# Where GpSimd subtracts the first feed-forward weights inside a tile of the first attention

## The chip, the cores and the metric

The kernel runs on one core of one Trainium2 chip. The metric is the device time of one execution in microseconds (us). The core has TensorE (PE, matrix products and transposes), VectorE (DVE), ScalarE (ACT), GpSimd (POOL) and SyncE (SP, which here issues most DMAs). Each engine runs its own instructions in order. Engines meet only through semaphores.

## The reference, cut to what matters

The network has four parts, each added to the residual `x` of 2048 rows by 512 columns. The change lies in the first, and the weights that it prepares belong to the second:

```
features_n = rmsnorm(features, fn_w)                 # features: ctx, 2048 x 512
Q = text @ Wq_w.T + Wq_b ;  K = features_n @ Wk_w.T + Wk_b
Q, K = rmsnorm(Q, qn_w), rmsnorm(K, kn_w)            # x += softmax(Q K^T * scale) features_n
inter = xf @ c1_w.T @ c2_w.T                         # second part: the largest of each 32 is chosen
h = relu(w1[chosen] . xf) ;  x += h @ w2t[chosen]
```

Products are made in about twice the precision of one pass: each operand is held as a high and a low part, and three products are added, high by high, low by high and high by low. So every operand needs a low part, which is the raw value minus its high part. `w1`, the first weights of the second part, are 128 x 7168 numbers in the laid-out form. They are split in eight pieces of 128 x 896 while the first attention runs.

## The kernel before, in words

The first attention goes over 16 tiles of 128 rows (n = 0 to 15). In tile n the engines finish the scores of tile n and prepare tiles n+1 and n+2. The instruction order of each engine is written out by hand in a `body(n)` for each. No scheduler moves anything.

A tile turns around the key of the next tile, as follows.

- TensorE projects the key and the query of tile n+1 (lines 72 to 74, 24 products of 512 columns), makes the scores of tile n (12 products), transposes rows (L881), attends for tile n-1, transposes the query (L907) and then the key (L913), and the probabilities (L969).
- VectorE adds the key bias (L688, into `kb`), the query bias (L692), makes scores and their maximum (L715, L717), and then `scale_keys` (L696): `kn = kb * krs * wqk`. Its two large inputs `kb` (in `a_wide`) and `wqk` (in `shared`) both lie in SBUF. `krs` is one number per row. L913 transposes `kn`, so it waits for L696.
- ScalarE makes the sum of squares of the key (L532), the exponentials (L579) and the high parts, those of `w1` at L560 and L564, one piece in each of tiles 7 to 14. L499 makes sums of squares for later roots.
- GpSimd makes the three roots of a tile (`tile_roots`, L400, L402, L406), the low part of the transposed features (L416), the key root `krs` (`key_root`, L379 and L381), then waits for `kn` (`s_kn`). After that come the low part of the features (`features_lo`, L411, which reads `cw` and `f_hi`), the weighting of the features (`weigh`, L374) and, in tiles 8 to 15, one subtraction of a piece of `w1` (`split_w1`, L456: 128 x 896 out of two SBUF inputs, float32 minus float16). Tile 9 has two small root instructions for a later layer norm (L114, L116) ahead of `features_lo`.

In tiles 8 to 13 the subtraction L456 is the last instruction of GpSimd's tile. In tile 14 it stands behind the wait for `kn` and ahead of `features_lo`. In tile 15 it follows the roots, since that tile has no key of a next one. Piece s is subtracted in tile s + 8, and its high part was made by ScalarE in tile s + 7.

In the trace tile 8 starts on GpSimd at 102.92 us and the last subtraction of `w1` ends at 170.12 us. The rest of the program, up to 1487 us, follows in order.

Of the kernel before, what the change touches and what calls it, by code (L numbers as in the profile page):

```python
# [33 lines left out]
NT = ROWS // P  # L34
# [155 lines left out]
def l0_attention(nc, ctx, big_ctx, m, prep, fw, a):  # L190
# [82 lines left out]
    SPLIT_AT = {n: n - 7 for n in range(7, 15)}  # L273
# [82 lines left out]
    def pool_steps(pool):  # L356
# [11 lines left out]
        def weigh(n):  # L368
            pool.wait_ge(c_in_, (n + 1) * 16)
            if n:  # L370
                pool.wait_ge(s_fl, n)
            else:
                pool.wait_ge(bq_fnw_in, 32)
            pool.tensor_tensor(cw[:, :], craw[:, bass.ts(n % 2, D)], fnw, ALU.mult).then_inc(s_cw, 1)  # L374
# [3 lines left out]
        def root(out, mean, down, eps, done):  # L378
            pool.tensor_scalar(out, mean, down, eps, ALU.mult, ALU.add).then_inc(s_rve, 1)  # L379
            pool.wait_ge(s_rve, next(roots))  # L380
            pool.tensor_tensor(out, out, m.neg_half[:, 0:1], ALU.pow).then_inc(done, 1)  # L381
# [11 lines left out]
        def tile_roots(n):  # L393
            pool.wait_ge(s_qss, n + 1)
            pool.wait_ge(s_css, min(n + 3, NT))
            pool.wait_ge(s_ve, 2 * min(n + 4, NT))
            if n >= RING:
                pool.wait_ge(s_pTl, n - 1)
            three = root4[:, n % RING, :]
            pool.tensor_tensor(three, sums[:, 1:4], eps3[:, :], ALU.add).then_inc(s_rve, 1)  # L400
            pool.wait_ge(s_rve, next(roots))
            pool.tensor_tensor(three, three, m.neg_half[:, 0:3], ALU.pow).then_inc(s_rve, 1)  # L402
            pool.wait_ge(s_rve, next(roots))
            if n >= 2:
                pool.wait_ge(s_xn, min(n + 2, NT))
            pool.tensor_scalar(sh2[:, (n + 3) % 2:(n + 3) % 2 + 1], sums[:, 0:1], -1.0, three[:, 0:1], ALU.mult, ALU.mult)\  # L406
                .then_inc(s_root, 1)

        def features_lo(n):
            pool.wait_ge(s_f, n + 1)  # L410
            pool.tensor_tensor(f_lo[:, bass.ts(n % F_RING, D)], cw[:, :], f_hi[:, bass.ts(n % F_RING, D)],  # L411
                               ALU.subtract).then_inc(s_fl, 1)

        def features_T(n):
            pool.wait_ge(s_cTh, n + 1)
            pool.tensor_tensor(cT_lo[:, :, :], cT_raw[n % 2][:, :, :], cT_hi[:, :, :], ALU.subtract).then_inc(s_cTl, 1)  # L416

        def key_root(n):
            pool.wait_ge(s_kss, n + 1)
            if n:  # L420
                pool.wait_ge(s_kn, n)
            root(krs[:, :], kss[:, :], 1.0, L0_EPS, s_krs)

        def body(n, first=False, ahead=True, project=True):
            if first:
                key_root(1)
            tile_roots(n)
            if ahead:
                features_T(n + 2)
            if first:  # L430
                weigh(1)
            if project:
                if not first:
                    key_root(n + 1)
                pool.wait_ge(s_kn, n + 2)
            if n == ROOT_AT:
                prep.pool_rstd(pool, 0)
            if n == NT - 2:
                split_w1(SPLIT_AT[n - 1])
            if project:  # L440
                features_lo(n + 1)
            if ahead:
                weigh(n + 2)
            if n - 1 in SPLIT_AT and n != NT - 2:
                split_w1(SPLIT_AT[n - 1])
            if n == C_AT:
                split_c1()
            if n == C_AT + 1:
                split_c2(0)
            if n == NT - 1:  # L450
                split_c2(1)

        def split_w1(s):
            cols = bass.ts(s, W1P // 2)
            pool.wait_ge(w1h_ok, s + 1)
            pool.tensor_tensor(fw.w1_lo[:, cols], w1_piece(s), fw.w1_hi[:, cols], ALU.subtract).then_inc(w1l_ok, 1)  # L456
# [15 lines left out]
        def split_c1():  # L472
            pool.wait_ge(ch_ok, 1)
            pool.tensor_tensor(fw.c1_lo[:, :, :], fw.c1_raw[:, :, :], fw.c1_hi[:, :, :], ALU.subtract).then_inc(cl_ok, 1)

        def split_c2(half):
            cols = bass.ts(half, INTER // 2)
            pool.wait_ge(ch_ok, 2)
            pool.wait_ge(cl_ok, half + 1)
            if half:  # L480
                pool.wait_ge(w1l_ok, 8)
            else:
                pool.wait_ge(s_cw, C_AT + 4)
            pool.tensor_tensor(fw.c2st[64:96, cols], fw.c2_raw[64:96, cols], fw.c2st[64:96, cols], ALU.subtract)\
                .then_inc(cl_ok, 1)
            pool.wait_ge(cl_ok, half + 2)

        run(body)(pool)

    def act_steps(act, before_exps):  # L490
# [2390 lines left out]
```

## Time and profile before

| | us |
|---|---|
| median of 3 runs (lowest, highest) | 1486.43 (1485.72, 1488.51) |
| the profiled execution | 1488.97 |
| its span, first to last instruction | 1487.2 |
| PE busy | 1456.9 (98%) |
| DVE busy | 1121.6 (75%) |
| ACT busy | 793.4 (53%) |
| POOL busy | 708.2 (48%) |
| mean granted TensorE clock | 0.999 of full speed |

The 1.8 us between the profiled execution's time and its span lie before the first and behind the last instruction. The shares are those of the whole span. The change touches a stretch of about 68 us out of 1487, and what its instructions wait for has to be read in that stretch.

### The profile page before, as it was taken

How to read it: one execution, taken by the hardware profiler on the slowest of the kernel's cores; microseconds unless marked ns; L12 is line 12 of the kernel's file. 1: busy time of each engine (PE TensorE's matmuls, PEld its weight loads, DVE VectorE, ACT ScalarE, POOL GpSimd, SP SyncE). 2: the span in 40 equal slices, each digit the busy share in tenths (PEclk: the TensorE clock that was granted, in tenths of full speed). 3: DMA queues.
4: the chain of work that ended last, by engine and by line, in shares of the span. 5: the costliest groups of instructions: out<-in, count | busy, mean ns of one | idle time of the engine just before them, and what ended most of it. 6: DMA issues, size and time to landing. Idle time of an engine off the chain costs nothing.

```text
span 1487.2 us, 27765 instructions
## 1 busy us (share of the span) xinstructions
PE 1456.9 (98%) x9948; PEld 851.1 (57%) x9948; DVE 1121.6 (75%) x2161; ACT 793.4 (53%) x3201; POOL 708.2 (48%) x668
## 2 busy tenths in 40 slices
PE   8999999999999989999999999999999999999998
PEld 6888645555555555556555555655555565555554
DVE  5887787888877878676776776777677677677868
ACT  5678731211123776565556646655754664565663
POOL 6678885554665453344233434333343433343553
PEclk9999999999999999999999999999999999999999
DMA  5744445443444585534443543543454345234523
GB/s 191 239 150 141 128 90 116 106 94 82 75 82 72 118 167 90 125 86 76 110 79 66 108 99 54 102 89 78 89 93 89 82 84 106 51 66 70 103 48 114
DMA packets 359225, 148.98 MB, mean 100 GB/s; under 512 B 342336, under 2 KB 342720, under 8 KB 356144
## 3 DMA queue, kind: packets, MB, share of 16 engines
q1 hardware_dynamic: 357792, 139.87, 44.2%
q10 hardware_dynamic: 1296, 7.34, 1.5%
q8 instruction: 79, 1.29, 0.4%
q14 instruction: 58, 0.48, 0.1%
HBM read 60.11 MB, written 4.19 MB: 43 GB/s over the span
## 4 chain that ended last, share of the span: by engine, by line
PE 49%; DVE 6%; ACT 5%; POOL 3%; DMA 2%; SPq 1%; issue 1%; DVEq 0%; POOLq 0%; ACTq 0%
PE bank L72 16%; PE bank L73 15%; PE bank L74 15%; ACT a_prob L1977 3%; PE bank L2649 2%; DMA a_kT_lo<-a_kn_lo 2%; ACT a_oT_lo L1954 1%; POOL a_qrs L1849 1%; DVE a_oT_lo L2246 1%; ACT a_qr_hi L1951 1%; POOL a_prob L1831 1%; DVE a_kn L2201 1%; DVE a_qve L2185 1%; DVE x_res L2169 1%; DVE x_res L2333 1%
## 5 line engine op out<-in xcount | busy, mean ns | idle before, releaser
L1977 ACT ACTIVATE a_prob<-a_prob,a_nmx 128x64 f32<-128x64 f32 x512 | 170.2, 334 | 250.0 <-DVE a_nmx L2222 249.9
L1831 POOL TENSOR_TENSOR a_prob<-a_prob,a_mask 128x512 f32<-128x512 f32 x64 | 79.9, 1269 | 278.4 <-DVE a_prob L2216 278.4
L72 PE MATMUL bank<-w,xT_hi 128*128 128x448 f16 (+1 forms) x512 | 187.5, 366 | 1.1 <-PEq L1043 1.1
L74 PE MATMUL bank<-w,xT_hi 128*128 128x448 f16 (+1 forms) x512 | 187.3, 366 | 0.0
L73 PE MATMUL bank<-w,xT_lo 128*128 128x448 f16 (+1 forms) x512 | 187.2, 366 | 0.0
L1849 POOL TENSOR_TENSOR a_qrs<-a_qve,neg_half 128x8 f32<-128x8 f32 x64 | 104.2, 1645 | 138.9 <-DVE a_qve L2185 138.6
L1251 ACT CAST f_h_hi<-h 128x448 f16<-128x448 f32 x64 | 35.6, 563 | 207.2 <-DVE h L1325 207.1
L2169 DVE SCALAR_TENSOR_TENSOR x_res<-bank,a_oinv,x_res 128x512 f32<-128x512 f32 x128 | 95.4, 746 | 64.2 <-PE bank L74 64.2
L2174 DVE SCALAR_TENSOR_TENSOR a_qr_lo<-bank,a_qr_hi 128x512 f16<-128x512 f32 x128 | 87.9, 687 | 46.4 <-ACT a_oT_lo L1954 27.4
L1837 POOL TENSOR_TENSOR a_p_hi<-a_prob,a_rden 128x512 f16<-128x512 f32 x64 | 69.5, 1086 | 104.3 <-DVE a_rden L2230 104.3
L1189 POOL TENSOR_TENSOR f_h_lo<-h,f_h_hi 128x448 f16<-128x448 f32 x64 | 72.8, 1141 | 88.9 <-ACT f_h_hi L1251 88.9
L72 PE MATMUL bank<-w,a_cT_hi 128*128 128x256 f16 x384 | 104.7, 273 | 1.0 <-DVE a_qr_lo L2174 1.0
L73 PE MATMUL bank<-w,a_cT_lo 128*128 128x256 f16 x384 | 104.7, 273 | 0.0
L74 PE MATMUL bank<-w,a_cT_hi 128*128 128x256 f16 x384 | 104.7, 273 | 0.0
L1954 ACT ACTIVATE a_oT_lo<-bank 128x128 bf16<-128x128 f32 x400 | 103.8, 282 | 0.0
L72 PE MATMUL bank<-w,a_oT_hi 128*128 128x512 f16 x256 | 97.2, 380 | 0.8 <-DVE x_res L2169 0.8
L73 PE MATMUL bank<-w,a_xT_lo 128*128 128x512 f16 x256 | 97.5, 381 | 0.0
L72 PE MATMUL bank<-w,a_xT_hi 128*128 128x512 f16 x256 | 97.5, 381 | 0.0
L74 PE MATMUL bank<-w,a_xT_hi 128*128 128x512 f16 x256 | 97.4, 381 | 0.0
L72 PE MATMUL bank<-shared,a_oT_hi 128*128 128x512 f16 x256 | 97.2, 380 | 0.1
L1998 ACT ACTIVATE a_oT_hi<-bank 128x512 f16<-128x512 f32 x97 | 54.3, 596 | 80.1 <-PE bank L74 59.1
L73 PE MATMUL bank<-w,a_oT_lo 128*128 128x512 f16 x256 | 97.0, 379 | 0.0
(355 smaller groups left out, 4439.3 us busy)
## 6 DMA issues: line engine op xcount, KB each, us to landing
shared<-in_l_wq SPq DMA_DIRECT2D x8, 1024.0 KB, 4.9
shared<-in_l_wo SPq DMA_DIRECT2D x8, 1024.0 KB, 5.2
shared<-in_w ACTq DMA_DIRECT2D x8, 896.0 KB, 4.7
craw<-in_w SPq DMA_DIRECT2D x11, 512.0 KB, 3.8
a_wide<-in_l_ctxT SPq DMA_DIRECT2D x16, 256.0 KB, 4.0
x_res<-in_x SPq DMA_DIRECT2D x16, 256.0 KB, 4.4
shared<-in_ctx SPq DMA_DIRECT2D x16, 256.0 KB, 4.3
shared<-in_l_wkv SPq DMA_DIRECT2D x8, 512.0 KB, 4.0
```

What stands on the lines that cost most here:

```text
L72: pe.matmul(out, a_hi, b_hi, start=first, stop=False)
L73: pe.matmul(out, a_lo, b_hi, start=False, stop=False)
L74: return pe.matmul(out, a_hi, b_lo, start=False, stop=last)
L1189: pool.tensor_tensor(h_lo[:, quarter(q)], h[:, quarter(q)], h_hi[:, quarter(q)], ALU.subtract).then_inc(s_hl, 1)
L1831: pool.tensor_tensor(blocks(prob[u][:, :]), blocks(prob[u][:, :]), mask[:, :].unsqueeze(1).broadcast_to([P, NB, S]), ALU.add).then_inc(s_m ...
L1837: pool.tensor_tensor(blocks(p_hi[u][:, :]), blocks(prob[u][:, :]), share, ALU.mult).then_inc(s_ph, 1)
L1849: pool.tensor_tensor(qrs[:, half], qve[:, half], m.neg_half[:, half], ALU.pow).then_inc(s_qrs, 1)
L1954: ins = act.activation(scratch, q_banks[t][:, h * HD:(h + 1) * HD], ACT.Square, scale=SUM_DOWN, accum_out=qss[:, h % 2, t, h // 2:h // 2 + 1])
L1977: ins = act.activation(pt, pt, ACT.Exp, bias=nmx[:, col:col + 1], accum_out=den[:, col:col + 1])
L1998: ins = act.activation(oT_hi[:, u * NB:(u + 1) * NB, b * S:(b + 1) * S], blocks(pv_banks[u][b][:, :]), ACT.Copy, scale=OUT_DOWN)
L2169: dve.scalar_tensor_tensor(xt, banks[t % 2][:, :], oinv[i // NCH % 2][:, c:c + 1], xt, ALU.mult, ALU.add).then_inc(s_x, 1)
L2174: dve.scalar_tensor_tensor(qr_lo[:, t, :], q_banks[t][:, :], SUM_DOWN, qr_hi[:, t, :], ALU.mult, ALU.subtract).then_inc(s_ql, 1)
```

## The change

In tiles 8 to 14 GpSimd makes its subtraction of `w1` right behind the key root, ahead of the wait for `kn`. The piece, its operands and its size are the same. Tile 15 keeps its order. No other engine's code is changed.

```diff
             if project:
                 if not first:
                     key_root(n + 1)
+            if n - 1 in SPLIT_AT:
+                split_w1(SPLIT_AT[n - 1])
+            if project:
                 pool.wait_ge(s_kn, n + 2)
             if n == ROOT_AT:
                 prep.pool_rstd(pool, 0)
-            if n == NT - 2:
-                split_w1(SPLIT_AT[n - 1])
             if project:
                 features_lo(n + 1)
             if ahead:
                 weigh(n + 2)
-            if n - 1 in SPLIT_AT and n != NT - 2:
-                split_w1(SPLIT_AT[n - 1])
```

GpSimd's order in tile 11, one of the six tiles 8 to 13, before. In brackets are the semaphores that an instruction waits for: `a0_kn_ok` is `s_kn`, `a0_w1_hi_ok` says that the high part of `w1` is there.

```order
L379 TENSOR_SCALAR a_krs<-a_kss 128x1 [waits a0_kn_ok,a0_kss_ok]
L381 TENSOR_TENSOR a_krs<-a_krs,neg_half 128x1 [waits a0_root_input]
L411 TENSOR_TENSOR a_big<-a_wide,a_big 128x512 [waits a0_f_ok,a0_kn_ok]
L374 TENSOR_TENSOR a_wide<-shared 128x512 [waits a0_f_lo_ok,a0_ctx_in]
L456 TENSOR_TENSOR w<-shared,w 128x896 [waits a0_w1_hi_ok]
L400 TENSOR_TENSOR a_root<-a_sums,a_eps 128x3 [waits a0_ln_var_steps,a0_pT_ok,a0_css_ok,a0_qss_ok]
```

The same place in the changed kernel, where the lines behind the change are numbered one lower:

```order
L379 TENSOR_SCALAR a_krs<-a_kss 128x1 [waits a0_kn_ok,a0_kss_ok]
L381 TENSOR_TENSOR a_krs<-a_krs,neg_half 128x1 [waits a0_root_input]
L455 TENSOR_TENSOR w<-shared,w 128x896 [waits a0_w1_hi_ok]
L411 TENSOR_TENSOR a_big<-a_wide,a_big 128x512 [waits a0_f_ok,a0_kn_ok]
L374 TENSOR_TENSOR a_wide<-shared 128x512 [waits a0_f_lo_ok,a0_ctx_in]
L400 TENSOR_TENSOR a_root<-a_sums,a_eps 128x3 [waits a0_ln_var_steps,a0_pT_ok,a0_css_ok,a0_qss_ok]
```

The subtraction moved from behind L374 to directly behind L381, and the wait for `kn` now stands behind it, on L411. In tile 14 GpSimd's order before was this:

```order
L379 TENSOR_SCALAR a_krs<-a_kss 128x1 [waits a0_kn_ok,a0_kss_ok]
L381 TENSOR_TENSOR a_krs<-a_krs,neg_half 128x1 [waits a0_root_input]
L456 TENSOR_TENSOR w<-shared,w 128x896 [waits a0_w1_hi_ok,a0_kn_ok]
L411 TENSOR_TENSOR a_big<-a_wide,a_big 128x512 [waits a0_f_ok]
L400 TENSOR_TENSOR a_root<-a_sums,a_eps 128x3 [waits a0_ln_var_steps,a0_pT_ok,a0_css_ok,a0_qss_ok]
```

Now it is this:

```order
L379 TENSOR_SCALAR a_krs<-a_kss 128x1 [waits a0_kn_ok,a0_kss_ok]
L381 TENSOR_TENSOR a_krs<-a_krs,neg_half 128x1 [waits a0_root_input]
L455 TENSOR_TENSOR w<-shared,w 128x896 [waits a0_w1_hi_ok]
L411 TENSOR_TENSOR a_big<-a_wide,a_big 128x512 [waits a0_f_ok,a0_kn_ok]
L400 TENSOR_TENSOR a_root<-a_sums,a_eps 128x3 [waits a0_ln_var_steps,a0_pT_ok,a0_css_ok,a0_qss_ok]
```

Here only the wait moved, from the subtraction to the instruction behind it.

## Rows read from the trace of the kernel before

**Rows 1.** Busy time in tile 12: us, then busy us of each engine.
```profile
142.80:152.30 9.50, 9.50 (x58) 8.17 (x57) 7.80 (x15) 8.92 (x20) 7.77 (x10) 1.00 0.36 104
```

**Rows 2.** Waits between 95 and 172 us: total, times, longest.
```profile
PE bank L913 <- DVE a_wide L696: 3.0, 4, 1.2
```

**Rows 3.** Timeline of tile 12: start, duration, engine, line [idle before it].
```profile
144.48 0.56 POOL L381 TENSOR_TENSOR a_krs<-a_krs,neg_half 128x1 f32<-128x1 f32 x1
...
145.08 0.75 DVE L696 SCALAR_TENSOR_TENSOR a_wide<-a_wide,a_krs,shared 128x512 f32<-128x512 f32 x1
...
145.34 0.60 PE L907 MATMUL bank<-ident,a_wide 128*128 128x128 f32 x4
...
145.88 0.66 PE L913 MATMUL bank<-ident,a_wide 128*128 128x128 f32 x4
145.91 1.28 POOL L411 TENSOR_TENSOR a_big<-a_wide,a_big 128x512 fp32r<-128x512 f32 x1 [0.86 <-DVE a_wide L696]
...
150.87 0.20 POOL L400 TENSOR_TENSOR a_root<-a_sums,a_eps 128x3 f32<-128x3 f32 x1 [0.36 <-issue]
```

**Rows 4.** Line 1319, all 64: duration ns min/median/max.
```profile
L1319 DVE TENSOR_TENSOR a_wide<-a_wide x64: 624/626/1252, 178.9 to 477.3; 128x448 bf16<-128x448 bf16 x64
```

**Rows 5.** Timeline of GpSimd and VectorE near 180 us.
```profile
179.12 2.53 POOL L1183 TENSOR_TENSOR f_w_lo<-shared,f_w_hi 128x1024 f16<-128x1024 f32 x1
...
180.87 1.25 DVE L1319 TENSOR_TENSOR a_wide<-a_wide 128x448 bf16<-128x448 bf16 x1
```

**Rows 6.** Line 851, all four: duration ns min/median/max.
```profile
L851 DVE TENSOR_TENSOR a_big<-x_res,a_big x4: 680/682/1786, 11.2 to 16.8; 128x512 fp32r<-128x512 f32 x4
```

**Rows 7.** Timeline of GpSimd at the start of the program.
```profile
16.39 1.67 POOL L416 TENSOR_TENSOR a_big<-a_wide,a_big 128x512 fp32r<-128x512 f32 x1 [1.42 <-ACT a_big L524]
...
22.97 0.55 POOL L381 TENSOR_TENSOR a_first_crs<-a_first_crs,neg_half 128x1 f32<-128x1 f32 x1
23.49 1.27 POOL L374 TENSOR_TENSOR a_wide<-shared 128x512 f32<-128x512 f32 x1
...
28.49 0.20 POOL L400 TENSOR_TENSOR a_root<-a_sums,a_eps 128x3 f32<-128x3 f32 x1
28.77 1.22 POOL L402 TENSOR_TENSOR a_root<-a_root,neg_half 128x3 f32<-128x3 f32 x1
...
37.98 0.86 POOL L402 TENSOR_TENSOR a_root<-a_root,neg_half 128x3 f32<-128x3 f32 x1
```

**Rows 8.** Timeline of VectorE at the start of the program.
```profile
28.51 0.75 DVE L696 SCALAR_TENSOR_TENSOR a_wide<-a_wide,a_krs,shared 128x512 f32<-128x512 f32 x1 [1.51 <-POOL a_krs L381]
```

**Rows 9.** Timeline of tile 9, GpSimd and VectorE.
```profile
115.15 0.56 POOL L381 TENSOR_TENSOR a_krs<-a_krs,neg_half 128x1 f32<-128x1 f32 x1
...
115.82 0.74 DVE L696 SCALAR_TENSOR_TENSOR a_wide<-a_wide,a_krs,shared 128x512 f32<-128x512 f32 x1
...
116.64 1.01 POOL L114 TENSOR_TENSOR ln_rs<-ln_ve,neg_half 128x4 f32<-128x4 f32 x1 [0.94 <-DVE a_wide L696]
...
120.58 1.92 POOL L456 TENSOR_TENSOR w<-shared,w 128x896 f16<-128x896 f32 x1
```

**Rows 10.** Timeline of tiles 10 and 11, the places that had slack.
```profile
126.17 0.75 DVE L696 SCALAR_TENSOR_TENSOR a_wide<-a_wide,a_krs,shared 128x512 f32<-128x512 f32 x1 [0.77 <-POOL a_krs L381]
...
126.98 0.66 PE L913 MATMUL bank<-ident,a_wide 128*128 128x128 f32 x4 [1.23 <-DVE a_wide L696]
...
131.10 0.20 ACT L499 ACTIVATION_READ_ACCUMULATOR shared<-shared 128x1 f32 x1
...
131.86 0.20 POOL L400 TENSOR_TENSOR a_root<-a_sums,a_eps 128x3 f32<-128x3 f32 x1
...
136.37 0.66 PE L913 MATMUL bank<-ident,a_wide 128*128 128x128 f32 x4 [0.27 <-DVE a_wide L696]
```

**Rows 11.** Timeline of tile 14 and the start of tile 15.
```profile
162.06 0.56 POOL L381 TENSOR_TENSOR a_krs<-a_krs,neg_half 128x1 f32<-128x1 f32 x1
...
162.85 0.74 DVE L696 SCALAR_TENSOR_TENSOR a_wide<-a_wide,a_krs,shared 128x512 f32<-128x512 f32 x1
```

## The prediction

> **What bounds the kernel now.** I read the engines' shares first, then the busy time by stretch, then the waits of the stretch that the change touches, and last its timeline. TensorE is busy for 1456.9 of 1487.2 us, so outside the changed stretch there is nothing for GpSimd to win. Inside it TensorE is the bound as well: in tile 12 it is busy for 9.50 of 9.50 us [rows 1], and GpSimd for 7.77. Yet TensorE waits for `kn` before it can transpose it (L913), 3.0 us in 4 tiles [rows 2].
>
> The timeline of tile 12 shows the ring on which all hangs [rows 3]. GpSimd ends the key root at 144.48 + 0.56 = 145.04. VectorE starts `scale_keys` (L696) at 145.08 and ends it at 145.83. TensorE starts L913 at 145.88, at the moment when L907 (145.34 + 0.60 = 145.94) is just through. So L696 has no slack: whatever makes it late makes TensorE idle by as much. GpSimd is idle for 0.86 us in just this time and runs L411 when L696 is through.
>
> **What the change removes.** The subtraction fills that idle time. GpSimd's tile gets shorter by about 0.9 us, as L411 and L374 come later but the tail of 1.9 us is gone. What could this give to TensorE? The roots of the next tile (L400) start in tile 12 only after a wait of 0.36 us for another engine [rows 3], so there GpSimd isn't late. It is late at tiles 10 and 11: TensorE waits 1.23 and 0.27 us at L913 [rows 10]. Of the 1.23 about 0.87 would go, since the root of tile 10 could start when L456 no longer ends tile 9 (120.58 + 1.92 = 122.50 against about 121.6) [rows 9]. Then the 0.27. If nothing else happened the gain would be 0.87 + 0.27 = 1.1 us, and tiles 12 to 15 would move forward by that, with TensorE full.
>
> **What the change adds.** L456 reads two SBUF operands. L696 reads two as well. Before, they never ran together, since GpSimd waited for `kn` in between. What happens when two such instructions meet can be read in this trace. Of the 64 L1319 on VectorE (both inputs in SBUF) the median takes 626 ns and the longest 1252 [rows 4]. One that took 1.25 us started at 180.87 while L1183, a GpSimd subtraction, ran from 179.12 to 181.65, and it ended at 182.12, 0.47 behind GpSimd [rows 5]. That is the whole duration less 0.15: it did nearly all its work after GpSimd was through. L851, the closest in size to L696 (128 x 512, two SBUF inputs), takes 682 ns, but 1786 ns for the one that started at 16.8 [rows 6], beside a GpSimd subtraction from 16.39 to 18.06 [rows 7]. It ended at about 18.61, 0.55 behind GpSimd, which is again its duration less 0.13. And L696 holds GpSimd off in its turn: L402 takes 0.86 us, but 1.22 beside the L696 of 28.51 [rows 7, 8]. I take from these rows that the later one waits for the earlier one's end, and then needs its own duration less 0.14.
>
> For L696 behind a subtraction of 1.92 us [rows 9] the end then is GpSimd's end + 0.75 - 0.14 = + 0.61. With T the end of the key root, the subtraction starts at T - 0.03 (L374 started at 23.49, L381 before it ended at 23.52 [rows 7]) and ends at T + 1.89. So L696 ends at T + 2.50. Before it ended at T + 0.79 in tile 12 [rows 3], and alike in tiles 8 and 13.
>
> This is the price: 1.71 us in a tile where L696 follows at once. The Trainium skill has this as a rule ("SBUF — State Buffer", section "Who interferes with whom"): a VectorE instruction with two SBUF inputs contends with a GpSimd one that reads SBUF, whoever issues first has the port for the whole instruction, and the other fully blocks. By the rule the sum is the one below. Read as a port that is shared by halves it would be about half as much. The 1.25 and 1786 ns rows speak for the rule.
>
> **The sum, tile by tile.** The shift is that of L913 on TensorE.
>
> - Tile 8: + 1.71, as in tile 12. The rest of VectorE, ScalarE and TensorE in the tile follows.
> - Tile 9: T moves by about 1.61, since the key's squares are late. L696 ended at T + 0.85 (115.82 + 0.74 against 115.15 + 0.56) [rows 9], and now at T + 2.50. Shift 1.61 + 1.65 = 3.26.
> - Tile 10: here GpSimd was late and TensorE idle. GpSimd's chain from L114 to the root of tile 10 takes 120.58 - 116.64 = 3.94 us [rows 9]. L114 now starts at 119.9, the root at about 123.9 instead of 122.5, and T comes 1.5 later, near 127.6. L696 ended at 126.92 [rows 10], and now ends at about 130.2. Shift 3.3. This tile adds nothing, because its old gap of 1.23 us is swallowed.
> - Tile 11: the root waited for GpSimd until 131.86, and now for ScalarE's 131.30 + 3.3 = 134.6. T moves by 2.8, and L696 ends 2.8 + 1.71 = 4.5 later [rows 10].
> - Tiles 12 and 13: + 1.71 each, to 7.96. Here T and VectorE depend on ScalarE and TensorE, which moved along.
> - Tile 14: L696 ended at 162.85 + 0.74 = 163.59 = T + 0.97 [rows 11]. Now + 1.53. It stands ahead of the scores here, so scores, exponentials, the probabilities and the last tile follow, and the sum is 9.5.
>
> Below zero the bound of this unknown is the 1.1 us of gain. Above it is a delay of the full 1.92 in all seven tiles, 13.4 us. I take 9.5, because L696 and L851 are alike in size and form.
>
> **What hides beside other work.** The piece's high part is a tile old, so the subtraction waits for nothing. `weigh` ends some 2.6 us later in the tile, but the roots of the next had 0.36 us of idle and now come 1.71 later anyway. The two DMA loads that wait for freed pieces of `w1` start earlier or move along. In tile 9 L114 and L116 come later; their result isn't read before tile 10's end. Behind tile 15 the feed-forward part starts with the shift and nothing gives it back, since TensorE is full there. Contention with other VectorE instructions changes little: the others in the stretch read PSUM or one SBUF operand.
>
> **Rivals.**
>
> 1. VectorE wins the race. In tiles 8, 10, 12 and 13 L696 can start at T + 0.04, just when the subtraction begins to read. If L696 wins, it isn't late at all and GpSimd is late by some 0.6 us instead, which it has to spare. L400 started at 28.49 and L696 at 28.51 [rows 7, 8], and L400 kept its 0.20 us, so a lead of 0.02 was enough for GpSimd. The subtraction's lead is 0.07. Still, L400 is tiny. Where VectorE arrives later (tile 9 at T + 0.11, tile 14 at T + 0.23) it loses in any case, and after tile 9 it arrives late in tile 11 too: 1.65 + 1.6 + 1.53 = 4.8 us, 1491.2.
> 2. They share. If the two slow each other instead of one blocking, L696 takes 0.75 more, 7 x 0.75 = 5.2 less about 0.7 in tile 10: 4.5 us, 1490.9. The 1786 ns of L851 speak against it.
> 3. No contention, GpSimd only gets shorter. This is the other side: 1.1 us faster, 1485.3, within what can be told from no change. It decides if L696 keeps its 0.75 us beside the subtraction, which no row excludes for this pair but rows 5 to 8 speak against. More than 3 us faster would need idle time on TensorE that the stretch doesn't have: its waits at L913 are 3.0 us in all [rows 2].
> 4. More than 9.5: the delay in tile 14 runs through to the start of the feed-forward part or tile 10 doesn't swallow its gap: up to 12 us, 1498.4.
>
> **How the numbers follow.** The profiled execution took 1488.97 us, and with 9.5 it would take 1498.5. It was 2.5 above the median of the runs, 1486.43. From the median the forecast is 1495.9. A measurement of this kernel can tell about 0.2%, 3 us, from no change. Chances: the forecast (8 to 11 us) 0.56, rival 1 0.14, rival 2 0.07, rival 3 0.12, rival 4 0.11. The range leaves out rival 3 and the bound of 13.4 us: 1490.0 to 1498.5. The likeliest one's own range is 1494.4 to 1497.4. Slower by over 3 us: 0.56 + 0.11 and nearly all of rivals 1 and 2, 0.86. The same: rival 3 and a little of 1 and 2, 0.13. Faster: 0.01.
>
> **What would show it.** In the changed profile seven of the 16 L696, those of tiles 8 to 14, are recorded with 2.2 to 2.5 us instead of 0.75, and the other nine are unchanged. L455 keeps 1.9 us. TensorE has a wait of 1.2 to 1.8 us for L696 at L913 in each of these tiles but tile 14, where it stands before L72 or L969. GpSimd's wait at L411 is still there. The last attention product ends about 9.5 us later. L696 at 0.75 and L455 at 2.5 us would be rival 1. L696 at 1.5 would be rival 2. Both unchanged would be rival 3, and would prove me wrong.

## The result, and the profile after

| us | before | changed |
|---|---|---|
| median of 6 runs each | 1487.16 (1485.33 to 1488.76) | 1496.83 (1493.81 to 1497.92) |
| ratio | | 1.0062, 95% interval 1.0048 to 1.0076 |
| profiled execution, its span | 1488.97, 1487.2 | 1497.7, 1495.8 |

The change makes the kernel 9.7 us slower, with an interval of 7.1 to 11.3. The forecast was 9.5. How much of this agreement is earned is told further down.

The timeline of tile 12 in the changed kernel (start, duration, engine, line) answers to [rows 3]:

```profile
149.84 0.56 POOL L381 TENSOR_TENSOR a_krs<-a_krs,neg_half 128x1 f32<-128x1 f32 x1
...
150.36 1.89 POOL L455 TENSOR_TENSOR w<-shared,w 128x896 f16<-128x896 f32 x1
150.43 2.37 DVE L695 SCALAR_TENSOR_TENSOR a_wide<-a_wide,a_krs,shared 128x512 f32<-128x512 f32 x1
...
150.70 0.60 PE L906 MATMUL bank<-ident,a_wide 128*128 128x128 f32 x4
...
152.85 0.33 PE L912 MATMUL bank<-ident,a_wide 128*128 128x128 f32 x1 [1.55 <-DVE a_wide L695]
152.87 1.29 POOL L411 TENSOR_TENSOR a_big<-a_wide,a_big 128x512 fp32r<-128x512 f32 x1 [0.63 <-DVE a_wide L695]
```

`scale_keys` (now L695) is recorded with 2.37 us instead of 0.75. It ends 0.55 us behind the subtraction, which keeps its 1.9 us. TensorE, which had no gap here, waits for 1.55 us. GpSimd's idle time hasn't gone either: it waits 0.63 us behind the subtraction for the same `kn`.

The busy time of that tile, and TensorE's waits for `kn` between 95 and 182 us, answer to [rows 1] and [rows 2]:

```profile
146.20:157.30 11.10, 9.55 (x57) 8.17 (x56) 8.93 (x14) 8.91 (x20) 7.75 (x9) 1.00 0.29 91
```

```profile
PE bank L912 <- DVE a_wide L695: 8.8, 7, 2.1
```

The tile takes 11.1 us instead of 9.5, with the same 9.5 us of work on TensorE. TensorE's waits for `kn` rose from 3.0 to 8.8 us.

### The profile page after: what moved, and what is told of

Read it like the earlier page. It is cut to its first block, busy times and chain, and to the rows that moved or that the text cites. A ratio compares the mean times of both kernels' runs of the same rounds, so it can differ in the third digit from the quotient of the medians.

```text
span 1495.8 us, 27765 instructions
## 1 busy us (share of the span) xinstructions
PE 1461.1 (98%) x9948; PEld 854.4 (57%) x9948; DVE 1128.7 (75%) x2161; ACT 792.3 (53%) x3201; POOL 707.5 (47%) x668
## 4 chain that ended last, share of the span: by engine, by line
PE 55%; DVE 5%; ACT 3%; POOL 2%; DMA 1%; SPq 1%; issue 0%; DVEq 0%; POOLq 0%; ACTq 0%
PE bank L72 17%; PE bank L74 17%; PE bank L73 17%; PE bank L2648 3%; ACT a_prob L1976 2%; DMA a_kT_lo<-a_kn_lo 1%; DVE a_oT_lo L2245 1%; ACT a_oT_lo L1953 1%; DVE x_res L2332 1%; DMA a_pT_lo<-a_p_lo 1%; DVE a_kn L2200 0%; POOL a_qrs L1848 0%; POOL a_prob L1830 0%; DVE a_qve L2184 0%; DVE a_p_lo L2233 0%
## 5 line engine op out<-in xcount | busy, mean ns | idle before, releaser
L72 PE MATMUL bank<-w,a_oT_hi 128*128 128x512 f16 x256 | 97.2, 380 | 0.8 <-DVE x_res L2168 0.8
L72 PE MATMUL bank<-shared,a_oT_hi 128*128 128x512 f16 x256 | 97.2, 380 | 0.0
L74 PE MATMUL bank<-w,a_oT_hi 128*128 128x512 f16 x256 | 97.1, 379 | 0.0
L74 PE MATMUL bank<-shared,a_oT_hi 128*128 128x512 f16 x256 | 97.1, 379 | 0.0
```

The source lines that it names most:

```text
L72: pe.matmul(out, a_hi, b_hi, start=first, stop=False)
L74: return pe.matmul(out, a_hi, b_lo, start=False, stop=last)
```

## The experiments

### The same order, but behind the wait

```diff
             if project:
                 pool.wait_ge(s_kn, n + 2)
             if n - 1 in SPLIT_AT:
                 split_w1(SPLIT_AT[n - 1])
```

> The changed kernel with one line moved: GpSimd waits for kn first and makes its subtraction of w1 after that, still ahead of features_lo. Order theory (the subtraction is bad where it stands, because it makes features_lo, weigh and the roots behind them later): as slow as the changed kernel, 1495 to 1498 us. Port theory (it is bad because it runs beside scale_keys): scale_keys is back at 0.75 us in all 16 tiles, GpSimd is idle for 0.86 us as before, and the time is that of the kernel before, 1486 to 1488 us.

Measured: 1487.16 us against 1487.05, ratio 1.0002 (0.9994 to 1.0011). The timeline of tile 12 on VectorE and GpSimd:

```profile
145.13 0.75 DVE L695 SCALAR_TENSOR_TENSOR a_wide<-a_wide,a_krs,shared 128x512 f32<-128x512 f32 x1
...
145.96 1.90 POOL L455 TENSOR_TENSOR w<-shared,w 128x896 f16<-128x896 f32 x1 [0.87 <-DVE a_wide L695]
```

The whole loss is gone though the subtraction still comes ahead of `features_lo`. So making `features_lo` and `weigh` later by a subtraction costs nothing that this run can tell (its interval is -0.9 to 1.6 us). The roots aren't tested by it: GpSimd's tile is as long as before, and they start where they did. What costs is that the subtraction runs beside `scale_keys`.

### The key in PSUM, so that `scale_keys` has one large SBUF input

```diff
+    key_of = lambda n: bk_bank[:, :] if n else kb
...
-            act.activation(sq, kb[:, :], ACT.Square, ...)
+            act.activation(sq, key_of(n), ACT.Square, ...)
-            dve.scalar_tensor_tensor(kb[:, :], bk_bank[:, :], crs(n), bk, ...)
+            dve.scalar_tensor_tensor(key_of(n), bk_bank[:, :], crs(n), bk, ...)
-            dve.scalar_tensor_tensor(kn[:, :], kb[:, :], krs[:, :], wqk, ...)
+            dve.scalar_tensor_tensor(kn[:, :], key_of(n), krs[:, :], wqk, ...)
```

> The changed kernel with the biased key (kb) of tiles 1 to 15 kept in the PSUM bank that it was made from, so that scale_keys reads one large SBUF input (wqk) and not two; GpSimd's subtraction stays right behind the key root. Port theory (two SBUF inputs against a GpSimd read): scale_keys takes 0.75 us beside the subtraction, and the time falls by 8 to 11 us, to 1485 to 1488. A theory by which any VectorE instruction is held off by a long GpSimd one, or the order is at fault: scale_keys keeps 2.4 us, the time stays at 1495 to 1498.

Measured: 1485.42 us against 1487.05, ratio 0.9991 (0.9982 to 1.0000). Tile 12 again:

```profile
143.07 1.91 POOL L456 TENSOR_TENSOR w<-shared,w 128x896 f16<-128x896 f32 x1
...
143.14 0.75 DVE L696 SCALAR_TENSOR_TENSOR a_wide<-bank,a_krs,shared 128x512 f32<-128x512 f32 x1
```

The two start 0.07 us apart, as in the changed kernel, and neither is held off. For `scale_keys` the only difference is where one of its inputs lies. The instructions that write the key and square it use PSUM here too; the control below tells what that is worth. The run is also what rival 3 had described, a gain from a shorter GpSimd tile. The forecast of that gain was 1.1 us, and the median shows 1.6, with an interval of 0 to 2.7.

### The control: the kernel before, with the key in PSUM

The same edit on the kernel before.

> The kernel before, with the biased key (kb) of tiles 1 to 15 kept in PSUM, as in the run with the changed kernel. It is the control for that run: nothing runs beside scale_keys here, so the port theory expects no change, 1486 to 1488 us, and scale_keys at 0.75 us. If keeping the key in PSUM is itself worth something (a shorter scale_keys or key squares), this run is faster too, by 1 us or more.

Measured: 1487.43 us against 1487.15, ratio 1.0002 (0.9993 to 1.0011). Keeping the key in PSUM is by itself worth nothing that can be told (-1.0 to 1.6 us), and its trace has TensorE's waits of before.

### Half a piece

```diff
             if n - 1 in SPLIT_AT:
-                split_w1(SPLIT_AT[n - 1])
+                split_half(SPLIT_AT[n - 1], 0)      # 128 x 448
...
             if ahead:
                 weigh(n + 2)
+            if n - 1 in SPLIT_AT:
+                split_half(SPLIT_AT[n - 1], 1)
```

> The changed kernel, but only the first half of each piece (128 x 448) is subtracted behind the key root and the other half at the tile's end, in tiles 8 to 15. Blocking theory: scale_keys is late by the length of what is ahead of it, so by about 0.95 us less than in the changed kernel: 1.4 us instead of 2.37, and 7 tiles give about 3.5 to 5 us over the kernel before, 1490 to 1492. A theory by which meeting at all has a fixed price: scale_keys stays at 2.4 us and the time at 1495 to 1498.

Measured: 1491.08 us against 1487.05, ratio 1.0028 (1.0019 to 1.0037), so 4.0 us. Tile 12:

```profile
145.93 1.04 POOL L459 TENSOR_TENSOR w<-shared,w 128x448 f16<-128x448 f32 x1
...
146.00 1.52 DVE L706 SCALAR_TENSOR_TENSOR a_wide<-a_wide,a_krs,shared 128x512 f32<-128x512 f32 x1
```

GpSimd's part ahead is 0.85 us shorter, and `scale_keys` is 0.85 us shorter too (1.52 instead of 2.37). It again ends 0.55 us behind GpSimd. The price is set by the length of what is ahead.

### A short instruction ahead, so that VectorE is first

```diff
             if n - 1 in SPLIT_AT:
+                if project:
+                    pool.memset(pause[:, :], 0.0)   # 128 x 128
                 split_w1(SPLIT_AT[n - 1])
```

> The changed kernel with a memset of 128 x 128 numbers on GpSimd (some 0.2 us, it reads nothing) between the key root and the subtraction in tiles 8 to 14, so that scale_keys starts first where it is ready. First come, first served: scale_keys takes 0.75 us in tiles 8, 11, 12 and 13, where it starts 0.04 us behind the key root, and the subtraction takes about 2.5 us there. Where VectorE comes later (tiles 9 and 14) it is still held off, and the time is 1488 to 1491 us. If GpSimd has priority whoever is first, scale_keys stays at 2.4 us and the time at 1496 to 1498.

Measured: 1491.11 us against 1487.05, ratio 1.0030 (1.0019 to 1.0041), 4.1 us. The upper end of what was expected, 1491, is missed by 0.1. Tiles 9 and 11, first VectorE, then GpSimd:

```profile
115.48 2.45 DVE L698 SCALAR_TENSOR_TENSOR a_wide<-a_wide,a_krs,shared 128x512 f32<-128x512 f32 x1
...
136.43 0.75 DVE L698 SCALAR_TENSOR_TENSOR a_wide<-a_wide,a_krs,shared 128x512 f32<-128x512 f32 x1
```

```profile
115.49 1.89 POOL L458 TENSOR_TENSOR w<-shared,w 128x896 f16<-128x896 f32 x1
...
136.51 2.43 POOL L458 TENSOR_TENSOR w<-shared,w 128x896 f16<-128x896 f32 x1
```

In tile 11 VectorE starts 0.08 us ahead. It keeps its 0.75 us, and GpSimd pays 0.54. The same happens in tiles 8, 12 and 13. In tile 9 the recorded starts are 0.01 us apart and VectorE pays 1.7. In tiles 10 and 14 GpSimd's recorded start is the earlier one, and VectorE pays there too (2.05 and 2.37 us). So no engine has priority: whoever is there first runs through. The Trainium skill says the same ("SBUF — State Buffer", section "Who interferes with whom"): issue order, not the form of the operation, decides who blocks.

### Three tiles alone

The kernel before, with the subtraction moved in tiles 11, 12 and 13 only.

> The kernel before with the subtraction moved behind the key root in tiles 11, 12 and 13 alone. Port theory with the sizes measured in the changed kernel (scale_keys ends 2.40 us behind the key root instead of 0.79, so 1.6 us a tile, less TensorE's 0.27 of idle time in tile 11): 1.3 + 1.6 + 1.6 = 4.5 us over the kernel before, 1491 to 1492, and scale_keys at 2.37 us in just these three tiles. If most of the change's cost came from tiles 8 to 10 and the clock behind them, these three would cost under 2 us, 1487 to 1489.

Measured: 1494.47 us against 1488.79, ratio 1.0036 (1.0024 to 1.0048), 5.7 us with an interval of 3.6 to 7.1. `scale_keys` takes 2.36, 2.37 and 2.37 us in these three tiles. From the key root of tile 8 to that of tile 14 the trace has 167.56 - 106.99 = 60.57 us. In the kernel before it was 162.06 - 106.03 = 56.03. The difference, 4.54, is the sum that was expected. Behind this stretch the profile of this run shows a granted clock of 0.70 between 175 and 180 us, which comes on top with some 1.5 us (worked out further down). The median lies above the 1491 to 1492 us of the expectation, partly because the kernel before is some 1.6 us slower on this chip.

### TensorE kept busy in tile 8, and the changed kernel once more

The profile of the changed kernel shows something that the prediction doesn't have, a fall of the clock behind the wait of tile 8:

```profile
110.00:112.00 2.00, 1.54 (x8) 1.35 (x8) 1.97 (x5) 0.83 (x3) 1.37 (x2) 0.74 0.00 0
112.00:114.00 2.00, 2.00 (x6) 1.61 (x5) 1.95 (x6) 2.00 (x7) 1.20 (x1) 0.50 0.00 0
```

The third number from the end is the granted clock. 0.50 is the lower of its two levels, 1.2 GHz. It fell after TensorE had waited 2.1 us at L912.

```diff
             elif project:
                 q_T(n + 1)
+                if n == 8:
+                    stay_busy(16)
                 k_T(n + 1)
```

> The changed kernel with 16 dummy transposes on TensorE in tile 8 ahead of the key's transpose, where TensorE otherwise idles for 2.1 us. Clock theory (that idle time makes the granted clock of the next stretch fall, 0.86 between 104 and 113 us in the changed kernel's profile): the clock stays at 1.00 there, and the median is 1 to 2 us below the changed kernel's, 1494 to 1496. If the fall of the clock has nothing to do with the idle time: the same mean clocks and the same median as the changed kernel, 1496 to 1498.

> The changed kernel once more, beside the run with dummy transposes on the same chip: 1495 to 1498 us. Clock theory: executions with a lower mean clock are the longer ones, and the profile shows a fall behind tile 8. Otherwise the clock falls elsewhere or not at all, with the same median.

Measured: with the dummy transposes 1499.57 us (1497.96 to 1501.27), ratio 1.0081 (1.0067 to 1.0095). The changed kernel again 1498.25 us (1495.82 to 1500.40), ratio 1.0072 (1.0060 to 1.0085), both against 1487.15. The same stretch with the dummy transposes, and a later one of each kernel:

```profile
110.00:112.00 2.00, 2.00 (x10) 1.64 (x10) 1.97 (x6) 2.00 (x5) 1.83 (x2) 1.00 0.00 0
112.00:114.00 2.00, 2.00 (x11) 1.65 (x10) 1.92 (x10) 2.00 (x6) 0.97 (x2) 1.00 0.03 8
175.00:180.00 5.00, 5.00 (x22) 3.88 (x23) 2.24 (x5) 3.42 (x6) 4.72 (x4) 0.66 0.17 31
```

```profile
175.00:180.00 5.00, 4.77 (x17) 3.94 (x18) 2.01 (x5) 3.78 (x6) 4.65 (x5) 0.53 0.15 20
```

The first half of the clock theory holds: with TensorE busy the clock stays at 1.00 behind tile 8, and in the repeat without transposes it fell again (0.54 between 112 and 114 us). The second half fails: the median isn't lower, and both medians lie above what was expected. The traces tell part of why. Where the clock fell, VectorE reached `scale_keys` of tile 9 only 0.2 us ahead of the subtraction's end, and that tile paid 1.4 us with the slow clock. Where it didn't fall the tile paid 0.9 us with the blocked port. From tile 8's root to L912 of tile 14 the two differ by only 0.45 us. And the clock fell in both at the start of the feed-forward part.

The other sign that was expected of the repeat did come: the executions with a lower mean clock are the longer ones. In the first group of the changed kernel those at 0.994 and 0.995 took 1497.44 to 1497.92 us, those at 0.998 and 0.999 took 1493.81 to 1496.22. In the repeat it was 1498.25 to 1500.40 at 0.994 and 0.995, and 1495.82 and 1497.46 at 0.997 and 0.998.

### The version without the wait

`scale_keys` no longer contends when its key lies in PSUM. Then GpSimd's wait for `kn` is needed for nothing.

```diff
             if n - 1 in SPLIT_AT:
                 split_w1(SPLIT_AT[n - 1])
-            if project:
-                pool.wait_ge(s_kn, n + 2)
```

> The changed kernel with kb in PSUM, and without GpSimd's wait for kn, which nothing needs once scale_keys no longer contends. Port theory: scale_keys stays at 0.75 us, GpSimd no longer idles behind the subtraction, but TensorE is full from tile 11 on, so the time is that of the run with the wait, 1484 to 1487 us. If GpSimd still bounds the tiles, another 1 to 2 us go. If the wait also kept off other contention, the time rises to 1488 or more.

Measured: 1484.20 us (1482.65 to 1486.18) against 1487.15, ratio 0.9981 (0.9972 to 0.9990). This is faster than both kernels, by 2.9 us (1.5 to 4.2) and by some 12.6. The last one asks which edit is worth it. It is the kernel before in its own order, with the key in PSUM and without the wait.

> The kernel before in its own order (subtraction at the tile's end), with kb in PSUM and without GpSimd's wait for kn: it tells whether the gain of the run with the changed order, PSUM and no wait comes from the wait or from the order. If from the wait: 1484 to 1485 us, as there. If the early subtraction is needed for it: 1486 to 1487.5, as the kernel before.

Measured: 1486.67 us against 1488.79, ratio 0.9984 (0.9976 to 0.9993), a gain of 2.1 us (1.0 to 3.6). The time itself lies in the range that was expected if the early subtraction were needed. But the kernel before was slower on this chip, and the gain is what counts. So with the key in PSUM each edit alone brings about as much: the new place alone 1.6 us (0 to 2.7), the missing wait alone 2.1, both 2.9. The intervals overlap, so the medians don't rank the three. The traces say much the same. They are compared at the start of tile 15's scores, a place that comes at 166.70 us in the control with nothing but the key in PSUM. Here it is in the kernel before, with the new place alone, with the wait gone alone, and with both:

```profile
167.03 0.30 PE L72 MATMUL bank<-a_big 128*128 128x128 f32 x1 [1.37 <-DVE a_pT_lo L725]
```

```profile
165.06 0.30 PE L72 MATMUL bank<-a_big 128*128 128x128 f32 x1 [1.36 <-DVE a_pT_lo L725]
```

```profile
164.90 0.30 PE L72 MATMUL bank<-a_big 128*128 128x128 f32 x1 [1.37 <-DVE a_pT_lo L725]
```

```profile
164.44 0.30 PE L72 MATMUL bank<-a_big 128*128 128x128 f32 x1 [1.36 <-DVE a_pT_lo L722]
```

Either edit takes GpSimd's 0.86 us of idle time out of its tile, and with it TensorE's waits in tiles 10 and 11. With the wait gone TensorE doesn't wait for `kn` in tiles 8 to 14 at all. The only wait between 95 and 172 us is that of tile 7, where before there were four with 3.0 us [rows 2]. With both edits:

```profile
PE bank L910 <- DVE a_wide L693: 0.9, 1, 0.9
```

## Why the prediction was right, and where it wasn't

**The mechanism was right.** All seven L695 of tiles 8 to 14 meet a subtraction. In the tiles where VectorE comes in time (8, 11, 12, 13) they take 2.36 or 2.37 us, where 2.2 to 2.5 was forecast, and L455 keeps 1.9. In the other three VectorE comes later: it takes 1.90 us in tile 10, 1.93 in tile 14 and 0.80 in tile 9. So the sign "2.2 to 2.5 us in all seven" failed in three tiles, and TensorE's waits are 2.12, 0.99, 1.45, 1.55 and 1.55 us in tiles 8 and 10 to 13, with none in tile 9, instead of 1.2 to 1.8 in each. Late or not, `scale_keys` ends 0.55 us behind the subtraction. Rival 1, VectorE winning the race, came true only when a memset stood ahead. A lead of 0.06 to 0.07 us was enough for GpSimd, as the prediction had read from [rows 7, 8]. Rival 2, sharing, gave L696 1.5 us beside the whole piece; 2.37 us and GpSimd's unchanged 1.9 exclude it. The 1.52 us beside the half piece would fit sharing if it stood alone, but GpSimd's half takes 1.04 us there and 1.05 at the tile's end, where nothing holds it. Rival 3, no contention, is what happens with the key in PSUM.

**The sum.** I count from the key root of tile 8, the last instruction ahead of the change (106.03 us before, 107.45 after), because the changed profile was 1.4 us late before any edit took effect. The shift of L912:

| tile | forecast | profile after |
|---|---|---|
| 8 | 1.71 | 1.61 |
| 9 | 3.26 | 3.01 |
| 10 | 3.3 | 2.76 |
| 11 | 4.5 | 3.95 |
| 12 | 6.25 | 5.55 |
| 13 | 7.96 | 7.15 |
| start of tile 15's scores | 9.5 | 8.18 |

Three terms were mis-sized. L695 ends 2.40 us behind the key root and not 2.50: the subtraction starts 0.04 ahead of the root's end and takes 1.89, and L695 ends 0.55 behind it, where 0.61 was taken from L1319 and L851. That is 1.6 us a tile instead of 1.71. In tile 10 the old gap gave back 0.25 us, where the sum had 0.04 added:

```profile
128.66 1.89 POOL L455 TENSOR_TENSOR w<-shared,w 128x896 f16<-128x896 f32 x1
...
129.20 1.90 DVE L695 SCALAR_TENSOR_TENSOR a_wide<-a_wide,a_krs,shared 128x512 f32<-128x512 f32 x1
...
131.16 0.66 PE L912 MATMUL bank<-ident,a_wide 128*128 128x128 f32 x4 [0.99 <-DVE a_wide L695]
```

L912 waits 0.99 here, less than the 1.23 of before [rows 10]. And tile 14 cost 1.0 and not 1.53. The key root moved there by 6.87 us only, 0.28 less than L912 of tile 13, and L695 ended 2.41 us behind it instead of 0.97:

```profile
170.88 1.90 POOL L455 TENSOR_TENSOR w<-shared,w 128x896 f16<-128x896 f32 x1
171.39 1.93 DVE L695 SCALAR_TENSOR_TENSOR a_wide<-a_wide,a_krs,shared 128x512 f32<-128x512 f32 x1
```

Tile 9 was nearly right in size (1.40 us, 1.55 forecast) for a wrong reason. There the clock had fallen, VectorE came 1.6 us behind the key root, and L695 took only 0.80:

```profile
118.55 1.90 POOL L455 TENSOR_TENSOR w<-shared,w 128x896 f16<-128x896 f32 x1
...
120.20 0.80 DVE L695 SCALAR_TENSOR_TENSOR a_wide<-a_wide,a_krs,shared 128x512 f32<-128x512 f32 x1
```

Where the clock was kept up by dummy transposes, tile 9 cost 0.9 us and the whole stretch 7.8. So without the clock the sum of 9.5 was 1.7 too high.

**What the total owes to something else.** Up to the scores of tile 15 the change costs 8.18 us in the first profile and 8.24 in the repeat's. The medians differ by 9.7 (7.1 to 11.3) and by 11.1 (8.9 to 12.6). The first interval holds the 8.2, the second doesn't, so something comes on top. In the repeat's profile it can be seen: its feed-forward part starts 11.35 us late, behind 0.53 and 0.79 of the full clock between 175 and 185 us. From the scores of tile 15 to the first product of the feed-forward part it takes 5.69 us in the kernel before and in the changed one, where the clock stays at 1.00, and 8.80 in the repeat.

But this fall of the clock isn't the change's own. It is there in the profiles of three kernels that aren't slower than the kernel before: the one that waits first, the one with the new place and the key in PSUM, and the one without the wait in the old order. These are the kernel before and the one that waits first:

```profile
165.00:170.00 5.00, 3.63 (x27) 2.86 (x25) 3.73 (x9) 4.97 (x9) 4.82 (x6) 1.00 0.36 105
170.00:175.00 5.00, 5.00 (x26) 2.75 (x24) 2.03 (x5) 3.62 (x8) 4.60 (x5) 1.00 0.38 105
```

```profile
165.00:170.00 5.00, 3.64 (x23) 2.94 (x22) 3.11 (x9) 4.97 (x9) 4.82 (x6) 0.85 0.35 105
170.00:175.00 5.00, 5.00 (x21) 2.69 (x20) 1.92 (x4) 2.21 (x6) 4.60 (x5) 0.81 0.37 105
```

In each of these three the same piece of work takes 7.15 to 7.18 us instead of 5.69. So one such fall costs 1.4 to 1.5 us here, and the repeat had 3.1 us of it. Other falls come at other places: near 540 us in the kernel before too, near 10 us in both profiles of the changed kernel, and near 40 us in the first of them alone. The repeat, without the fall near 40 us, reaches tile 8 when the kernel before does, so that fall accounts for the first profile's 1.4 us.

Over the executions the mean granted clock is lower in the changed kernel: 0.9963 in its 11 executions (0.994 to 0.999), 0.9988 in the 21 of the kernel before beside the repeat (0.997 to 1.000). Within both groups of the changed kernel 0.001 less goes with some 0.6 us more. From this I estimate 1.6 us for the lower clock, which with 8.2 makes 9.8. By this estimate the number was hit because a sum 1.3 us too high stood in for a clock that the prediction had left out, and that is luck. That the changed kernel loses 8.2 us up to tile 15 is shown, 7.8 of it without the fall of the clock behind tile 8. That the rest is the clock is seen in one profile and estimated for the medians, and why it falls more often in the changed kernel stays open: with the dummy transposes the mean was 0.9964, no higher.

**What hides.** That later `features_lo` and `weigh` cost nothing was right, by the first experiment. The prediction took the 0.36 us ahead of the roots in tile 12 for a wait for another engine, while the row names none (`issue`) [rows 3]. In the run that waits first the same gap is put down to ScalarE's L498, which supports its reading. The gain if nothing contends, 1.1 us, was right in sign and too small: counted from the key root of tile 8, TensorE reaches the scores of tile 15 2.1 us earlier with the new place and the key in PSUM. The transpose of the key gains 0.2, 1.4 and 0.4 us in tiles 9, 10 and 11, where 0.87 and 0.27 were forecast for the last two. The median shows 1.6, with an interval of 0 to 2.7.

## What to carry to other kernels

Idle time of GpSimd is not free to fill if VectorE works there on two SBUF inputs: look at what VectorE runs in the gap and at where its operands lie, before anything is moved into it. If the two must meet, put one of VectorE's inputs in PSUM. To let VectorE be first helps only in the tiles where it is ready in time: with the memset the kernel was still 4.1 us slower. A wait that no data needs may be what keeps two engines apart. Take away the contention, and then the wait can go too, which here was worth about as much as the move.

## What the runs showed of the hardware

- The blocked one does nearly all of its work after the other one's end: 0.75 us of work ended 0.55 us behind GpSimd after 1.04 us and after 1.89 us alike. What counts is what GpSimd has left: where VectorE came 0.25 us ahead of its end, `scale_keys` took 0.80. The blocking GpSimd instruction wasn't longer (1.88 to 1.90 us beside VectorE, 1.90 to 1.93 in the kernel before).
- With one of its two large inputs in PSUM the same VectorE instruction takes 0.75 us beside the same GpSimd instruction, and neither is longer.
- The switch lies between a recorded lead of VectorE of 0.01 us (GpSimd ran through) and 0.08 us (VectorE ran through).
- GpSimd pays less when it loses: 2.43 us instead of 1.89, so 0.54, for 0.75 us of VectorE.
- A wait of 2.1 and 2.2 us on TensorE in tile 8 was followed by the lower clock in both profiles of the changed kernel, and by none when dummy transposes filled it. Waits of 1.5 to 1.6 us in tiles 11 to 13, and one of 1.88 in tile 11 of the run with three tiles, were not followed by it.
- The wait alone doesn't decide. Ahead of tile 15's scores TensorE waits 1.36 or 1.37 us in seven of these kernels. The clock fell behind it in four profiles (1.4 to 1.5 us lost) and stayed at 1.00 in three.
